# Block 2's keys and queries as three float32r products, with a new order of steps, in a kernel of two transformer blocks

## What is computed

```python
# block 1: 16 heads of width 8
x1 = layernorm(x + mha(x, x, Wq1, Wk1, Wv1, causal=True))      # "A"
x2 = layernorm(x1 + mha(x1, c, Wq2, Wk2, Wv2, causal=False))   # "B"
h2 = layernorm(x2 + relu(x2 @ fc1.T + b1) @ fc2.T + b2)
# block 2: 16 heads of width 64, "C"
q, k, v = h2 @ wq + bq, c @ wk + bk, c @ wv + bv
w   = softmax(q k^T / 8 + 2 * fs)                              # fs: (32, 16, 64, 64)
out = layernorm((w @ v) @ wo + bo + h2)
```

## Time and profile before

| | us |
|---|---|
| three runs | 413.66, 414.31, 415.24 (median 414.31) |
| the profiled execution, its own time | 412.68 |
| its span, first to last instruction | 410.8 |
| PE / DVE / ACT / POOL busy | 347.7 / 309.3 / 235.4 / 236.2 |
| mean granted TensorE clock | 0.969 |

### The profile page before, as it was taken

The page is one execution under the profiler, slowest core; times in us unless marked ns, Lnnn a source line. Parts: engine busy times, 40 slices in busy tenths (PEclk is TensorE's granted clock), DMA queues, the critical chain, the costliest instruction groups (busy, mean ns, idle before and its releaser), DMA issues.

```text
span 410.8 us, 13138 instructions
## 1 busy us (share of the span) xinstructions
PE 347.7 (85%) x5296; PEld 242.4 (59%) x5296; DVE 309.3 (75%) x897; ACT 235.4 (57%) x561; POOL 236.2 (57%) x372
## 2 busy tenths in 40 slices
...
DMA packets 13180, 17.87 MB, mean 44 GB/s; under 512 B 1600, under 2 KB 10176, under 8 KB 13120
## 3 DMA queue, kind: packets, MB, share of 16 engines
...
...
## 4 chain that ended last, share of the span: by engine, by line
PE 65%; ACT 15%; DVE 8%; issue 4%; POOL 3%; SPq 3%; DMA 2%; POOLq 0%; DVEq 0%
ACT qT L644 8%; PE C_E L535 8%; PE C_E L453 6%; PE C_E L467 6%; PE C_E L526 5%; PE C_E L488 4%; PE C_E L501 4%; PE A_E L362 4%; PE B_E L362 3%; PE B_E L395 3%; ACT A_S L566 2%; PE C_E L512 2%; PE A_X L381 2%; ACT PTc L661 2%; PE A_E L395 2%
## 5 line engine op out<-in xcount | busy, mean ns | idle before, releaser
L899 POOL TENSOR_TENSOR L_ve<-L_mv,cst 128x1 f32<-128x1 f32 x64 | 12.1, 190 | 80.3 <-DVE L_mv L802 80.2
L891 POOL TENSOR_TENSOR A_kblk<-A_qk,cst 128x1024 f32<-128x1024 f32 x16 | 30.3, 1896 | 37.8 <-DVE A_qk L732 37.8
L559 ACT COPY A_qk<-A_J 128x256 f32<-128x256 f32 x16 | 6.0, 372 | 71.8 <-PE A_X L369 67.0
L932 POOL TENSOR_TENSOR Sc<-Sc,mxc 128x512 f32<-128x512 f32 x32 | 33.3, 1042 | 18.6 <-DVE mxc L849 18.6
L644 ACT ACTIVATE qT<-C_E,bq 128x128 f32<-128x128 f32 x128 | 36.0, 369 | 11.4 <-PE C_E L488 11.4
L910 POOL TENSOR_TENSOR L_xg<-L_xh,vec_sb 128x128 f32<-128x128 f32 x64 | 29.1, 455 | 17.3 <-DVE L_xh L811 15.8
L901 POOL TENSOR_TENSOR L_rstd<-L_ve,cst 128x1 f32<-128x1 f32 x64 | 35.2, 549 | 5.0
L467 PE MATMUL C_E<-wv_sb,cTs 128*64 128x512 f32 x128 | 35.2, 628 | 0.8 <-DVE Sc L840 0.8
L941 POOL TENSOR_TENSOR Pc<-Pc,rdc 128x512 f32<-128x512 f32 x32 | 32.8, 1042 | 5.3 <-DVE rdc L859 5.3
L488 PE MATMUL C_E<-x3T,wq_sb 128*128 128x128 f32 x256 | 35.3, 281 | 0.4 <-ACT x3T L636 0.4
L535 PE MATMUL C_E<-wo_sb,C_zT 128*128 128x128 f32 x256 | 33.3, 286 | 1.6 <-ACT C_zT L631 1.4
...
## 6 DMA issues: line engine op xcount, KB each, us to landing
...
cs<-in_ctxn SPq DMA_DIRECT2D x1, 768.0 KB, 12.5
...
```

Of the source, the lines that this page charges most:

```text
L891: tt(a.kblk[:], a.qk[:, 1].unsqueeze(1).to_broadcast([P, 8, P]), at["rmask"].unsqueeze(2).to_broadcast([P, 8, P]), ALU.mult).then_inc(a.s_ ...
L932: tt(v, v, mxc[:, 8 * g:8 * g + 8].unsqueeze(2).to_broadcast([P, 8, S]), ALU.subtract).then_inc(C.s_sub, 1)
```

## The change

1. Keys: wk and c are split into a hi part (a copy rounded to float32r) and a lo part (the difference), and each key product becomes three float32r products: hi·hi, lo·hi and hi·lo. wk's split is done once (whi on ACT, wlo on DVE), c's once for a group of four pairs (chi on ACT, clo on POOL).
2. Queries: the same with wq (wqhi, wqlo) and with h2: x3_hi is the eviction of the transpose (ACT), x3_lo a new DVE step x3l.
3. bvo is moved in the order, from position -4.9 to -1.8. It now waits for the values of the pair before, and x3t of pair 0 waits for it instead of k_0.
4. x1 and h2 get six buffers each (RING = 6).
5. The order: TURN now gives each step a position as a number.

Parts of the diff (the renamed buffers of x1 and h2 are left out):

```diff
@@ bvo
                 pe.wait_ge(w_out, 16 * 2)
+                pe.wait_ge(C.s_vs, 2)
@@ c_k
-                    if j < 2 and group < 2:
-                        pe.wait_ge(s_cT[group], 16)
+                    if j == 0:
+                        pe.wait_ge(C.s_clo, group + 1)
                     if n == 0:
-                        pe.wait_ge(w_keys, 16 * 3)
-                        pe.wait_ge(bvo_ready, 2)
+                        pe.wait_ge(C.s_wlo, 1)
                     elif n < FIRST:
                         pe.wait_ge(C.s_ks, 2 * n - 1 + g)
                     else:
                         pe.wait_ge(C.s_s, 2 * (n - FIRST) + 1 + g)
-                    mm(C.E[g][:, :], wk_sb[:, j * P:(j + 1) * P], cTs[:, group * FIRST * P:(group + 1) * FIRST * P],
-                       start=True, stop=True).then_inc(C.s_k, 1)
+                    hi, lo = (w[:, j * P:(j + 1) * P] for w in (wk_hi, wk_lo))
+                    chi, clo = cT_hi[group % 2], cT_lo[group % 2]
+                    mm(C.E[g][:, :], hi, chi[:], start=True, stop=False)
+                    mm(C.E[g][:, :], lo, chi[:], start=False, stop=False)
+                    mm(C.E[g][:, :], hi, clo[:], start=False, stop=True).then_inc(C.s_k, 1)
@@ c_x3t
                 if n:
                     pe.wait_ge(L4.s_y, n)
-                tr(C.E[0][:, 0:P], h2[:], ident).then_inc(C.s_x3t, 1)
+                else:
+                    pe.wait_ge(bvo_ready, 2)
+                tr(C.E[0][:, 0:P], h2[n % RING][:], ident).then_inc(C.s_x3t, 1)
@@ c_q
-                    pe.wait_ge(C.s_x3ts, n + 1)
+                    pe.wait_ge(C.s_x3lo, n + 1)
+                    if n == 0:
+                        pe.wait_ge(C.s_wlo, 2)
...
                     for j in range(4):
-                        c = (4 * g + j) * P
-                        last = mm(C.E[g][:, j * P:(j + 1) * P], wq_sb[:, c:c + P], x3T[:], start=True, stop=True)
+                        c, to = (4 * g + j) * P, C.E[g][:, j * P:(j + 1) * P]
+                        mm(to, wq_hi[:, c:c + P], x3_hi[:], start=True, stop=False)
+                        mm(to, wq_hi[:, c:c + P], x3_lo[:], start=False, stop=False)
+                        last = mm(to, wq_lo[:, c:c + P], x3_hi[:], start=False, stop=True)
@@ ACT
+            def whi(n):
+                if n:
+                    return
+                act.wait_ge(w_keys, 16 * 3)
+                act.copy(wk_hi[:], wk_sb[:]).then_inc(C.s_whi, 1)
+
+            def wqhi(n):
+                if n:
+                    return
+                act.wait_ge(w_values, 16 * 2)
+                act.copy(wq_hi[:], wq_sb[:]).then_inc(C.s_whi, 1)
+
+            def chi(n):
+                if n % FIRST:
+                    return
+                if n in (0, FIRST):
+                    act.wait_ge(s_cT[n // FIRST], 16)
+                if n >= 2 * FIRST:
+                    act.wait_ge(C.s_k, 2 * (n - FIRST))
+                act.copy(cT_hi[n // FIRST % 2][:], cTs[:, n * P:(n + FIRST) * P]).then_inc(C.s_chi, 1)
@@ x3ts
-                act.copy(x3T[:], C.E[0][:, 0:P]).then_inc(C.s_x3ts, 1)
+                act.copy(x3_hi[:], C.E[0][:, 0:P]).then_inc(C.s_x3hi, 1)
@@ DVE
+            def wlo(n):
+                if n:
+                    return
+                dve.wait_ge(C.s_whi, 1)
+                tt(wk_lo[:], wk_sb[:], wk_hi[:], ALU.subtract).then_inc(C.s_wlo, 1)
+
+            def wqlo(n):
+                if n:
+                    return
+                dve.wait_ge(C.s_whi, 2)
+                tt(wq_lo[:], wq_sb[:], wq_hi[:], ALU.subtract).then_inc(C.s_wlo, 1)
+
+            def x3l(n):
+                dve.wait_ge(C.s_x3hi, n + 1)
+                tt(x3_lo[:], C.E[0][:, 0:P], x3_hi[:], ALU.subtract).then_inc(C.s_x3lo, 1)
@@ POOL
+            def clo(n):
+                if n % FIRST:
+                    return
+                pool.wait_ge(C.s_chi, n // FIRST + 1)
+                k = n // FIRST % 2
+                tt(cT_lo[k][:], cTs[:, n * P:(n + FIRST) * P], cT_hi[k][:], ALU.subtract).then_inc(C.s_clo, 1)
@@ TURN
+C.loadf=-10.6806663 C.store=-9.6806686 A.qkv=-6.5177677 A.qk=-6.2676461 A.e0=-6.1161541 A.q0=-6.0941994
...
```

More of the change, by code:

```diff
@@ L171, in norm @@
             return l
-        x1 = [sb(f"x1_{k}", [P, D]) for k in range(2)]
-        h2 = sb("h2", [P, D])
+        x1 = [sb(f"x1_{k}", [P, D]) for k in range(RING)]
+        h2 = [sb(f"h2_{k}", [P, D]) for k in range(RING)]
         x2 = sb("x2", [P, D])
@@ L191, in bass_two_blocks @@
         f = [sb(f"f{k}", [P, H * S]) for k in range(2)]
+        cT_hi, cT_lo = ([sb(f"{n}{k}", [P, FIRST * P], F32R) for k in range(2)] for n in ("cT_hi", "cT_lo"))
+        wk_hi, wk_lo, wq_hi, wq_lo = (sb(n, [P, HD], F32R) for n in ("wk_hi", "wk_lo", "wq_hi", "wq_lo"))
         kT = [sb(f"kT{k}", [P, J, FIRST * P]) for k in range(2)]
@@ L194, in bass_two_blocks @@
         zT = sb("C_zT", [P, 2, J // 2, P])
-        x3T, x3r, qT = sb("x3T", [P, P]), sb("x3r", [P, D]), sb("qT", [P, J, P])
+        x3_hi, x3_lo = sb("x3_hi", [P, P], F32R), sb("x3_lo", [P, P], F32R)
+        x3r, qT = sb("x3r", [P, D]), sb("qT", [P, J, P])
         Sc, Pc = sb("Sc", [P, H * S]), sb("Pc", [P, H * S])
@@ L200, in bass_two_blocks @@
         C.s_k = sem("C_k")
+        C.s_chi, C.s_clo, C.s_whi, C.s_wlo = (sem("C_" + n) for n in ("chi", "clo", "whi", "wlo"))
         C.s_ks = sem("C_ks")
@@ L959 @@
 TURN = """
-B.pv_0+2 C.den_0+1 B.gb+2 C.qs_1+1 C.den_1+1 C.sub_0+1 A.sub_0+5 B.qk+3 B.pv_1+2 A.qk+6 C.ks_0+5 C.bvo+5 C.q_0+1
-B.z+2 C.q_1+1 B.qkv+3 C.exp_0+1 C.e+1 A.max_1+5 A.nz+6 A.qkv+6 C.ks_1+5 A.sub_1+5 C.sub_1+1 B.max_0+3 B.max_1+3
-C.exp_1+1 B.sub_0+3 B.y3+2 B.e0+3 C.vs_0+2 A.e+5 B.3st+2 C.vs_1+2 B.kblk+3 B.cnt+3 B.f1s+2 A.exp_0+5 C.nrm_0+1
-B.f2s+2 B.sub_1+3 C.k_0+5 C.nrm_1+1 C.k_1+5 B.am+4 B.3xh+2 C.pts_0+1 C.v_0+2 A.gb+4 B.3rstd+2 C.x3c+1 A.cut+6
-A.v+6 C.y+1 A.exp_1+5 B.f1+2 C.pts_1+1 C.st+1 A.m0+5 A.pts_0+5 A.zn+5 A.e0+6 A.y+5 A.pts_1+5 C.v_1+2 B.e+3
@@ L965 @@
-B.f2+2 C.pt_0+1 C.pt_1+1 B.f3+2 B.exp_0+3 B.3gb+2 A.kblk+6 A.pt_0+5 C.zts_0+1 C.zts_1+1 B.exp_1+3 B.cm+4 A.zts+5
-A.cnt+6 A.st+5 B.pts_0+3 B.pts_1+3 A.pt_1+5 C.gb+0 B.zn+3 B.y+3 C.zt+1 C.x3ts+2 B.st+3 B.q0+4 B.xts+4 C.xh+1
-A.pv_0+5 A.pv_1+5 B.pt_0+3 B.zts+3 A.xh+5 B.xh+3 C.o_0+1 C.o_1+1 C.rstd+1 C.fadd_0+2 A.rstd+5 B.pt_1+3 C.max_0+2
-B.nz+4 B.tr+4 C.obias+6 C.loadf+5 B.rstd+3 C.qs_0+2 A.z+5 C.fadd_1+2 C.max_1+2 C.store+4 B.cut+4 A.max_0+6
-C.x3t+2 A.q0+7 B.v+4
+C.loadf=-10.6806663 C.store=-9.6806686 A.qkv=-6.5177677 A.qk=-6.2676461 A.e0=-6.1161541 A.q0=-6.0941994
@@ new lines @@
+A.cnt=-5.9761320 A.nz=-5.8770845 A.kblk=-5.8116963 A.m0=-5.7854553 A.cut=-5.7709955 A.v=-5.7022353
+C.clo=-5.5917326 C.chi=-5.4802263 A.e=-5.4273537 C.k_0=-5.3877125 C.k_1=-5.3671361 C.whi=-5.3179630
+C.ks_0=-5.2461882 A.pt_0=-5.2132076 A.exp_0=-5.2008420 A.max_0=-5.1676581 C.wlo=-5.1614419 A.exp_1=-5.1223169
+A.pt_1=-5.1054918 A.max_1=-5.0942017 C.ks_1=-5.0826492 A.sub_0=-5.0245230 A.sub_1=-4.9837098 A.pts_0=-4.9218418
+A.pv_0=-4.8499971 A.pv_1=-4.7702961 A.zn=-4.6879683 A.pts_1=-4.6280678 A.y=-4.6207246 A.rstd=-4.5964749
@@ new lines @@
+A.st=-4.5884002 A.zts=-4.5783065 A.gb=-4.5777865 A.z=-4.5574458 A.xh=-4.3754216 B.am=-3.8264371 B.tr=-3.6099649
+B.cm=-3.5935222 B.q0=-3.5883975 B.qkv=-3.5500415 B.e0=-3.4848888 B.xts=-3.4763399 B.nz=-3.4454799
+B.kblk=-3.4452033 B.cnt=-3.4303314 B.qk=-3.4171311 B.e=-3.3656860 B.cut=-3.2804618 B.v=-3.2671469
+C.wqhi=-3.1487691 B.pt_0=-2.9960179 B.max_0=-2.9656277 B.exp_0=-2.9626708 B.sub_0=-2.9619029 B.max_1=-2.9074713
+B.exp_1=-2.8669463 B.sub_1=-2.8618181 B.pt_1=-2.8497242 B.pv_0=-2.7381179 C.wqlo=-2.7295398 B.pts_0=-2.6438033
```

52 lines of the change are left out of this document (39 added, 13 removed).

## The result

The changed kernel takes **436.75 us** (median of four runs, 433.74 to 438.25) against 413.99 us for the kernel before, measured beside it: ratio 1.054, interval 1.048 to 1.060. The forecast was 405 us with a range of 390 to 424, so it has the wrong sign, and the result lies outside the range. The profile is of the fastest of the four (433.74 us).

What follows compares the result with a forecast made beforehand. PE was taken as the bound, DVE close behind and the floor after the change. Head -9.4, bvo +1.0, turns -0.6, fill +0.9, drain -1.0 sum to -9.1: from 412.68, 403.6 + 1.6 = 405 us, range 390 to 424.

Steps and rivals of the forecast that it cites:

- the price of the query products: Queries on PE, each turn: 24 float32r products take 1.3 us against 1.8 before, saving 0.45 us of PE.
- Rival 2: Weight loads bind the queries on PE: 2.7 us instead of 1.3, a turn 0.3 us longer, 409 us; chance 0.15.
- the walk of the turn: Engine queues stepped through one turn from C.y's start: fadd_0 at 7.3 us, keys at 8.05, turn 20.8, taken as 20.9.
- The order: Steady turns: DVE's queue before fadd_0 takes back what PE saves; 0.05 us less per turn, -0.6 us over twelve.
- rival 1: Steady turns: DVE's floor is reached, PE not held at the keys, turns 20.1 to 20.3 us, 396 us; chance 0.14.
- The keys: Key products on PE, each turn: 6 float32r products at 0.21 us, 1.3 us against 1.8, saving 0.5 us.
- The head: Start of the run: bvo later opens PE's queue, A's exponential starts at 19.3 us instead of 28.71, -9.4 us.
- The drain: Last turns: queries lose 0.45 us, x3_lo and hand-over gain 0.35, DVE's queue before fadd_0 is shorter; -1.0 us.
- Rival 3: Queries between x3_lo and energies: 128-column float32r products cost like float32 or the transpose, 448 or 426 us; chance 0.20.
- low ends: Lowest prices for float32r on PE, taken from bf16: 1.3 us a turn for keys and 1.3 for queries.
- the buffers: Six buffers for x1 and h2: no engine waits for them now, so alone they change 0.
- SP and for clo: SP's store ahead of a load, and POOL's clo waiting for chi: 0, with 1 us each if that cover goes.

Runs made afterwards that it cites:

- order_f32: The changed kernel with keys and queries both as float32 products again, leaving the order, later bvo and six buffers: 420.62 us, ratio 1.014 to the kernel before.
- old_k: The kernel before, in its old order, with later bvo, six buffers and float32r keys, queries in float32: 413.35 us, ratio 0.998.
- k_f32: The changed kernel with only the keys back in float32: 434.88 us, ratio 1.047 to the kernel before.
- q_f32: The changed kernel with only the queries back in float32, no wq split and no x3l: 418.36 us, ratio 1.008 to the kernel before.
- rates: The bench: the changed kernel followed by chains of independent matmuls, to read steps between starts; its own total time says nothing.
- ring: The kernel before with six buffers for x1 and h2 and nothing else: 415.12 us, ratio 1.001.

## Why the prediction was wrong

**The step that failed first: the price of the query products.** The forecast took the low end, 24 x 0.056 = 1.3 us, with bf16 as the row "of such a type". Measured: 24 at 0.11 = 2.7 us. The count of bits in the type speaks for the product, not for its weight load, and the row against it, the load at 191 ns in the earlier trace rows, was seen and named: in the changed kernel the loads are recorded at 191 and 192 ns, in the bench bf16's at 98. Rival 2 had this price right and its consequence wrong: for 1.4 us more of PE it moved the turn by 0.3 us, where the runs show 0.86 for 0.9 us more (2.7 against float32's 1.8), with 1.2 in the old order. So the price alone, put right, would not have saved the forecast: the walk of the turn failed too, in the three ways that follow.

**Why the longer queries reached the turn: the walk missed a link.** It let DVE do 5.84 us of work in one piece after x3_lo, so fadd_0 came at 7.3 us after c_y whatever PE did. But the first of that work after B.st is B.cut, which needs B.cnt, which stands on PE behind the queries. In the profile fadd_0 starts 8.45 us after c_y (121.83 - 113.38), 1.15 later, which is DVE's wait of 1.13 for L356. The walk listed B.cnt in PE's queue and B.cut in DVE's and did not join them. With queries 1.4 us shorter, as priced, B.cnt would have ended before DVE asked for it (an estimate: 118.46 - 1.4 = 117.06, where DVE's wait begins at 117.37), so the price and the link failed together. With B.cnt moved the cost of the queries in float32r falls from 0.86 to 21.82 - 21.32 = 0.50 us.

**The second half of the turn was summed short.** From the keys' start to the next c_y it had 12.75 us; the profile has 135.94 - 122.56 = 13.38. The walk's own PE work adds to 18.2 us (1.9 + 1.3 + 1.4 + 1.1 + 12.5), while the same text puts PE's need at 19.6. Had the two been compared, the missing work would have been seen. So 22.56 - 20.8 = 1.76 splits into 1.13 of DVE's wait and 0.63 of this sum.

**The order was taken as nearly free; it costs 1.05 us a turn.** The PE wait before the keys, named fadd's Sc, came as forecast (2 us said, 1.79 measured), but this is luck in its size: C.e before it ended 7.39 us after c_y (119.61 + 1.16 - 113.38), not 6.1, and fadd started 1.15 us late. That DVE's queue holds the keys was the right mechanism; that it only takes back what PE saves was not. With no new products at all (order_f32) PE waits 1.64 us there and the turn is 1.05 longer; the float32r keys take 0.33 off it and the queries add 0.86. DVE never became the floor (18.85 us busy of 22.57), so rival 1 is out.

**The keys** were sized nearly right: a product steps at 0.23 us, but the first of the six at 0.34, and from the first one's start to the next step PE takes 1.60 us (122.56 to 124.16), where the float32 keys of order_f32 take 1.92. So 0.32 us are saved, not 0.45; all of it reaches the turn here and none in old_k.

**The head** was forecast at -9.4, with +0.9 and +1.0 in the fill: -7.5 in all; -4.6 came. The first steps were met: the keys start at 17.89 us (17.9 forecast), held 2.15 us by wk_lo, and A's first exponential at 19.45 (19.3). A's energies start at 13.52, not 11.3: the products of A's next pair stand ahead of them on PE. This head is kept for four pairs, whose exponentials start 9.3, 8.6, 9.2 and 9.5 us earlier than before, and then 4.8 us of it are lost up to the first eviction, where +1.9 were forecast for the longer way and bvo. In order_f32, with both types in float32, the first eviction is at 66.57 us, 7.3 earlier than before. With the queries alone in float32r (k_f32) it is at 67.42, with the keys alone (q_f32) at 70.68, with both at 69.30. So it is the keys, their splits included, that cost in the fill, as in old_k; the forecast had them 2 us cheaper there. Their exact price stays open, because the granted clock falls at different times in these executions: in the changed kernel's it is 0.5 from 18.8 to 22.3, 29.1 to 32.5 and 46.2 to 49.6 us.

**The drain** was forecast at -1.0 and gave +3.3. In order_f32 its first two turns are 18.72 and 18.38 us against after's 19.62 and 19.28, again 0.9 us for the queries. In the last full turn the granted clock is 0.62, and the last 27 us have 0.56. The same three turns take 3.3 us less in rates, so part of this is the execution's and not the code's.

**Rival 3** named the right sign and the right place, "between x3_lo and the energies", but at the wrong price: it asked for 1.7 us over the low ends before a loss. 1.5 us (1.4 and 0.1) came, with a loss of 22.8 us. The point from which it decided was set by the same short walk, which held the order for free.

**Nothing for the buffers, nothing for SP and for clo**: the first is shown by ring; for the others no wait of an engine shows in the steady turns of the after profile.
